# Two layers of cross-attention on one core: statistics between maxima and sums, a projection behind the first keys, and the last MLP two slots on

## The reference

```python
# layer 0
n = layernorm(x, ln1);  q, k, v = heads16(n @ wqkv)
r = x + merge(softmax(causal(q k^T / sqrt(128))) v) @ wproj + bproj
q2 = heads16(layernorm(r, ln2) @ ed_wq);  k2, v2 = heads16(layernorm(ctx, ln2) @ ed_wkv)
r = r + merge(softmax(q2 k2^T / sqrt(128)) v2) @ ed_wproj + ed_bproj
x = r + relu(layernorm(x, ln3) @ ff_w1 + ff_b1) @ ff_w2 + ff_b2
# layer 1: 16 heads of 64; keys are 16 memory tokens, 16 persistent ones and the 56 rows
x = x + attention(rope(q), rope(k), v) @ to_out_w
h = rmsnorm(x) @ ff_w1 + ff_b1;  a, g = split(h)
x = x + (silu(g) * a) @ ff_w2 + ff_b2
```

## Time and profile before

| | |
|---|---|
| median of 3 runs | 1267.42 us (1264.57 to 1268.15) |
| the profiled execution's own time | 1259.12 us |
| its span, first to last instruction | 1256.5 us |
| TensorE busy, mean granted clock | 1122.8 us (89%), 0.965 |
| VectorE, GpSimd, ScalarE busy | 910.4, 837.2, 752.5 us |

### The profile page before, as it was taken

How to read it: one execution, slowest core, us unless ns; L and a number is a source line. 1 busy time by engine, 2 the same in 40 slices (tenths; PEclk the granted TensorE clock), 3 DMA queues, 4 the chain that set the end, 5 groups by cost and what they waited for, 6 DMA issues and landing times. The chain is left out here.

```text
span 1256.5 us, 38139 instructions
## 1 busy us (share of the span) xinstructions
PE 1122.8 (89%) x15980; PEld 757.1 (60%) x15980; DVE 910.4 (72%) x1730; ACT 752.5 (60%) x1077; POOL 837.2 (67%) x1235
## 2 busy tenths in 40 slices
PE   2888878999999999999999999999657699898985
PEld 1555645666666666666666666666442457575663
DVE  6788757887787887778877788777356768686813
ACT  1333476777777777777777777777612336363641
POOL 2687467887888878878788787871009887767400
PEclk9999888999999999999999999999979899999987
DMA  7200043232222323223223232121000000000000
GB/s 172 85 2 1 17 127 109 72 108 87 94 96 83 107 77 105 98 70 118 79 95 109 66 113 89 64 76 39 2 17 1 2 2 2 8 2 1 9 9 8
DMA packets 70790, 75.99 MB, mean 60 GB/s; under 512 B 21596, under 2 KB 65372, under 8 KB 70492
## 3 DMA queue, kind: packets, MB, share of 16 engines
q1 hardware_dynamic: 70620, 73.57, 18.8%
HBM read 32.89 MB, written 0.92 MB: 27 GB/s over the span
## 5 line engine op out<-in xcount | busy, mean ns | idle before, releaser
L1129 DVE TENSOR_REDUCE tops_sb<-ps_b 112x2 f32<-112x1000 f32 x378 | 453.3, 1199 | 151.9 <-PE ps_b L899 149.5
L1054 ACT ACTIVATE probs_sb<-ps_a 128x896 f32<-128x896 f32 x352 | 322.6, 916 | 118.5 <-PE ps_a L851 118.5
L842 PE MATMUL ps_d<-probs_sb,values_sb 128*32 128x112 f32 x6144 | 228.2, 266 | 0.6 <-ACT probs_sb L1054 0.5
L899 PE MATMUL ps_b<-keys_sb,queries_sb 64*112 64x500 f16 x756 | 160.8, 416 | 14.4 <-DVE tops_sb L1129 9.4
L226 POOL TENSOR_SCALAR context_sb<-context_sb,ln_sb 125x128 f32<-125x128 f32 x384 | 168.4, 456 | 7.7 <-POOL ln_sb L244 7.6
L842 PEld LDWEIGHTS ps_d<-probs_sb,values_sb 128*32 128x32 f32 x6144 | 135.0, 109 | 40.2 <-issue 7.2
L851 PEld LDWEIGHTS ps_a<-queries_sb,keys_sb 64*128 64x128 f16 x3072 | 125.1, 102 | 49.9 <-ACT probs_sb L1054 8.7
L851 PE MATMUL ps_a<-queries_sb,keys_sb 64*128 64x112 f16 x3072 | 141.0, 210 | 5.8 <-ACT probs_sb L1054 5.5
L867 PE MATMUL ps_c<-xs_t_sb,w_kv_sb 128*128 128x200 f32 (+1 forms) x384 | 123.6, 419 | 0.9 <-ACT xs_t_sb L1079 0.9
L938 PE MATMUL ps_c<-w_kv_sb,xs_t_sb 128*128 128x128 f32 x768 | 119.2, 292 | 1.1 <-ACT k_rows_sb L997 1.0
L761 POOL TENSOR_TENSOR k_split_sb<-k_rows_sb,k_split_sb 128x500 f16<-128x500 f32 x96 | 109.0, 1136 | 8.0
(11 more groups left out here) (267 smaller groups left out, 1902.6 us busy)
## 6 DMA issues: line engine op xcount, KB each, us to landing
keys_sb<-k_split_sb SPq DMA_DIRECT2D x288, 125.0 KB, 2.5
context_sb<-in_ctx SPq DMA_DIRECT2D x32, 750.0 KB
queries_sb<-q_split_sb SPq DMA_DIRECT2D x21, 112.0 KB, 5.8
keys_sb<-in_ones SPq DMA_DIRECT2D x3, 375.0 KB, 3.3
w_qk_sb<-in_w_qkv SPq DMA_DIRECT2D x1, 1024.0 KB, 11.5
queries_sb<-shift_sb SPq DMA_DIRECT2D x64, 1.8 KB
x_all_sb<-in_x SPq DMA_DIRECT2D x2, 448.0 KB
out<-y_sb SPq DMA_DIRECT2D x8, 112.0 KB
```

The costliest lines, as they stand in the source:

```text
L842: last = nc.tensor.matmul(o_bank[32 * (g % 4):32 * (g % 4) + 32, 112 * (g // 4):112 * (g // 4) + 112], values[r][:, k, g, :], probs[k % 2] ...
L899: last = nc.tensor.matmul(scan_of(b + d, n)[0:2 * T, 512 * e:512 * e + 500], queries_of(b + d, e, g), keys[(r + d) % 3][64 * e:64 * e + 64 ...
L1054: nc.scalar.activation(probs[s % 2][:].rearrange("p (e n) -> p e n", e=2), halves(ps_a[:, :]), ACT.Exp).then_inc(Q["probs_ready"], 1)
L1129: nc.vector.tensor_reduce(tops[(b + d) % 2][:, :, n // 3, n % 3], scan_of(b + d, n)[0:2 * T, :].rearrange("p (e n) -> p e n", e=2)[:, :, 0 ...
```

## The change

It does three things.

1. Stage 1: in each pass VectorE's statistics move from behind the normalised result to between the last row maximum and the first row sum.
2. Stage 2: in b = -2 `queries_made(0)` moves from ahead of slot 0 to slot 3 on TensorE, so behind the first three key products, and `queries_high(0)` moves on ScalarE from slot 2 to slot 5, behind all three `keys_out`. In b = -1 the scan of a slot now stands ahead of that slot's `rows_turn` or `queries_made`.
3. Stage 3: in the last round the MLP of round 2 runs two slots earlier (`EARLIER` = 2), on TensorE, ScalarE and VectorE.

```diff
@@ stage 1, VectorE, in the loop over passes
                                                         own_half.unsqueeze(1).unsqueeze(3).broadcast_to([128, 16 * U, 2, D0]),
                                                         ALU.mult).then_inc(S["v_ready"], 1)
+                        if i < 2:
+                            context_counted(i)
+                        else:
+                            rows_counted(2 * U * (i - 2), U * i)
+                        if i == NIT - 1:
+                            n = U * i
+                            rsqrt(ve, row_link, rstd[:, 0:n], meanvar[:, 0:n, 1], newton[:, 0:n], EPS0)
                         for u in range(U):
                             wait("e0_ready", u + 1)
                             ins = nc.vector.reduce_sum(s_sum[:, u, :], s0[u][:], AX.X)
...
-                        if i < 2:
-                            context_counted(i)
-                        else:
-                            rows_counted(2 * U * (i - 2), U * i)
-                        if i == NIT - 1:
-                            n = U * i
-                            rsqrt(ve, row_link, rstd[:, 0:n], meanvar[:, 0:n, 1], newton[:, 0:n], EPS0)
                         if i == NIT - 1:
                             rows_done(i)
@@ stage 2, TensorE
                         if b == -2:
                             rows_turn(0)
-                            queries_made(0)
                         for s in range(KT):
+                            if b == -2 and s == 3:
+                                queries_made(0)
+                            d = 2 if s in AHEAD else 1
+                            if has(d):
+                                scan(UNITS[s], d)
                             if b == -1 and s % 3 == 0 and s < 9:
                                 rows_turn(s // 3 + 1)
                             if b == -1 and s % 3 == 1 and s < 9:
                                 queries_made(s // 3 + 1)
-                            d = 2 if s in AHEAD else 1
-                            if has(d):
-                                scan(UNITS[s], d)
@@ stage 2, ScalarE
-                            if b == -2 and s == 2:
+                            if b == -2 and s == 5:
                                 queries_high(0)
-                            if b == -2 and s == 5:
                                 queries_low(0)
@@ stage 3
-            ROW_AT, Y_AT = 6, 15
+            ROW_AT, Y_AT, EARLIER = 6, 15, 2
@@ TensorE, and the same on ScalarE and (with mlp_normed) on VectorE
                             if i > 0:
-                                mlp(i - 1, n)
+                                mlp(i - 1, n + EARLIER * (i == NIT - 1))
```

More of the change, by code:

```diff
@@ L1749, in _ @@
                             if i > 0:
-                                mlp_normed(i - 1, n)
-                                mlp(i - 1, n)
+                                mlp_normed(i - 1, n + EARLIER * (i == NIT - 1))
+                                mlp(i - 1, n + EARLIER * (i == NIT - 1))
                     for n in range(16):
```

## The result

| | before | changed |
|---|---|---|
| median of 18 runs each, one chip | 1266.05 us | 1255.83 us |
| ratio, 95% interval | 1 | 0.9935 (0.9916 to 0.9954) |
| the changed kernel in a second comparison | 1 | 0.9913 (0.9881 to 0.9944) |
| profiled execution: its time, span, granted clock | 1259.12, 1256.5, 0.965 | 1257.92, 1256.0, 0.953 |

The two medians differ by 10.2 us; the ratio of 0.9935, which has the interval, makes 8.2. Weighted by their intervals the two comparisons make 0.9929 ± 0.0016, or 9.0 ± 2.1 us of 1266.

The account below looks back on a forecast made before the run. TensorE, busy 686 of 698 us, fills stage 2's full part, so time moves only in stage 1, the pipeline-filling calls and the end. 1.2 + 0.2 - 1.6 - 4.6 = -4.8 us, from 1267.42 to 1262.6; range 1258.5 to 1267.0.

Parts of the forecast that it names:

- The statistics, pass by pass: Stage 1: moving the statistics gains 1.3 us in passes 0 and 2 but costs in pass 1; sum +1.2 us.
- the keys of passes 1 and 3 released by ScalarE: Sign in stage 1: in the changed profile the widened keys there wait for ScalarE's copy.
- little idle time ahead of the sums: Sign in stage 1: VectorE idles no more than 0.7 us ahead of the fourth sum in passes 0 and 2.
- a wait of 6.98 us in pass 1: Sign in stage 1: VectorE idles some 6.9 us ahead of the twelve BN_STATS, released by GpSimd's last statistics instruction.
- Passes 0 and 2: Stage 1: keys start when they leave PSUM, statistics covered by idle time; -1.3 us each.
- The term for pass 1: Stage 1: VectorE's wait for GpSimd delays pass 2's scores; +2.5 us, between 1.5 and 4.0, pass 0's gain included.
- Queries and scans: Stage 2's filling calls: first queries +0.2 us, scans ahead of the rows in b = -1 -1.6 us.
- The last round: Stage 3: down projection starts 2.1 us earlier and runs 2.55 us faster at the full clock; -4.6 us.
- The slow down projection: Rival, last round: the down projection stays slow, giving 2.1 not 4.6; total -2.3 us, 1265.1; chance 0.21.
- the call b = -1: Rival, stage 2: the queries' own chain bounds this call, its 1.6 us falls away; total -3.2, 1264.2; chance 0.13.
- the long low clock in pass 2: Rival, stage 1: after pass 1's wait the low clock holds for all of pass 2; +4.7 us, 1272.1; chance 0.04.

Follow-up runs that it names:

- the kernel with ten products: Ten unread products put on TensorE into pass 1's wait for the normalised result, against the changed kernel; 0.9915 of before.
- the last round's kernel: Only the last round's MLP two slots earlier, against the kernel before; 0.9970 in the first run, 0.9940 in the second.
- balanced statistics: Changed kernel, statistics dealt out as first context, four rows, second context plus four rows; pass 3's behind the result: 0.9907 of before, 0.9891 with unread last-MLP products.
- the widening in turn: Kernel before with one wait more: GpSimd begins its share of the widened keys when VectorE has done its own; 1259.16 us, 0.9941.

## Why the prediction missed

**The statistics: the step that failed.** "The statistics, pass by pass" made +1.2 of them; alone they measure -2.8 ± 2.3, and between the down projections of pass 0 and pass 3 -2.64. The waits it named were right: the keys of passes 1 and 3 released by ScalarE, little idle time ahead of the sums (0.83 us in pass 0, just over the 0.7 named), a wait of 6.98 us in pass 1 (6.9 forecast). What was wrong is that it charged the low clock to the one wait that the change makes and put at nothing the low clock behind the waits that it shortens. Two gains were not in the sum.

- Passes 0 and 2 gain 1.94 us each (18.15 to 16.21), not 1.3. VectorE now comes to the widening just ahead of GpSimd, not in the midst of its row, and takes 2.14 instead of 2.82.
- The scores behind the waits. I had put the low stretch in pass 2's scores down and used it only for the price of the new wait; that the change would remove such stretches in the three passes stood nowhere. First scores to down projection fell from 11.68 to 10.63 on the mean, 3.2 us in three passes.

Together -1.94 - 1.94 - 3.2, and pass 1's 23.6 for a mean of 19.2, +4.4: -2.7, beside the -2.64 between the down projections.

The term for pass 1 came out by luck: the scores of pass 2 start 2.7 us later, for +2.5. The forecast let half of the chain behind the wait run low and gave 4.0 if all of it did. All of it did (0.50 from 88.00 to 94.60), but from the transposition to the scores that is 4.28 us and not the 5.4 that it had added up, since the rows overlap and the output projection takes 1.73, not 2.08; at the full clock, in the kernel with ten products, it is 2.36. And 0.65 of the 2.7 stands already at the down projection of pass 0 (44.31 for 43.66), ahead of the first widening that the change can bring forward. In the other three profiles of the new stage 1 the scores start 0.9 to 3.3 later than in before's.

**Queries and scans: right in kind, sized from a best case.** -1.4 forecast, -4.2 ± 2.1 measured in the time, -2.1 in the rows up to stage 3. In the profiles of before and after the two first scans lie 23.15 and 21.47 us apart, the forecast's 1.6. But the old order is dearer when the clock is low there, and the profile of before showed its best case. VectorE and then TensorE in the last round's kernel, second run, which has the old order here, and below them the granted clock of the stretch in that run and in the changed kernel:

```profile
184.85 1.20 DVE L1129 TENSOR_REDUCE tops_sb<-ps_b 112x2 f32<-112x1000 f32 x1 [1.48 <-PE ps_b L899]
188.78 1.20 DVE L1129 TENSOR_REDUCE tops_sb<-ps_a 112x2 f32<-112x1000 f32 x1 [2.73 <-PE ps_a L899]
```

```profile
183.13 1.09 PE L878 MATMUL ps_d<-const_sb,values_sb 128*128 128x128 f32 x4 [1.38 <-DVE values_sb L1098]
...
186.24 1.91 PE L884 MATMUL ps_d<-keys_sb,w_q_sb 128*128 128x512 f32 x2
```

```profile
172.00:199.00 27.00, 21.90 (x80) 10.97 (x81) 17.82 (x27) 16.27 (x33) 17.48 (x29) 0.68 0.30 96
```

```profile
170.60:192.20 21.60, 18.26 (x78) 9.46 (x78) 17.24 (x25) 15.59 (x31) 15.33 (x25) 0.78 0.38 119
```

Where a scan stands behind a transposition or a projection at 1.2 GHz (1.09 and 1.91 us, for 0.63 and 1.13 in the group after them), VectorE waits 1.48 and 2.73 us for it, for 0.78 and 1.13; the old order took 26.02 us at 0.68. The new one takes 21.47 at 0.78, below the 0.85 at which before's profile took 23.15. From the opening transposition to the first scan it is 15.54 in before's profile, but 17.3 to 18.1 in five of the eight with the old code; with the new one 15.0 to 15.8 in eight of ten, and 17.3 in the two with balanced statistics. Of all this 0.3 us is given back by the third element's first scan, and 2.2 at the end of stage 2.

**The last round: right.** 64.62 became 59.66 from the first values product to the end of the last output projection, -4.96 for -4.6: 2.1 from the slot, 2.55 from the down projection at full clock, 0.35 from the output projection, at full clock throughout (7.31 for 7.66). Behind it the last MLP ends another 0.65 us earlier (26.87 to 26.22), which I had called unchanged.

**The rivals.** The slow down projection did not come in any of the ten profiles with the new last round; the call b = -1 did what it is for up to the third element; the long low clock in pass 2 did not come: behind the 6.19 us wait it was over by the scores (1.09 us at 94.81). None of the rivals had more gain than the forecast. The sizes on that side came from one execution that stood 8.3 us below the median; I carried the difference over to the median and kept the sizes of a lucky run.

## What to carry to other kernels

In this kernel a wait on TensorE of 2.56 us or more cost its own length and, in 15 of 21 passes, another 1.6 us of scores at the low clock; when a change shortens a wait, count both, and count them in each place where it recurs. Measure a gain to the end of the stage behind it: a part of it can be lost where nothing was edited. Where a kernel's times scatter by more than the effect, one profile shows one draw: ask of each step how long it would take with the products in it at 1.2 GHz, and prefer the order in which the work that another engine waits for stands ahead of those products. Before adding work to an engine's idle time, look at what the other engines do at that moment: here one wait that keeps two engines apart was worth 7.5 us, the move of the statistics 2.8.

## What was unexpected of the hardware

VectorE and GpSimd hold each other up in the widening, and by how much depends on when VectorE arrives. The next rows give shortest, median and longest of two instructions of VectorE in ns: before in pass 1; the last round's kernel, first run, in pass 1; and with the widening in turn.

```profile
L596 DVE TENSOR_TENSOR k_wide_sb<-k_sb,const_sb x2: 1370/1448/1526, 89.1 to 90.4; 128x512 f32<-128x512 f32 x2
```

```profile
L596 DVE TENSOR_TENSOR k_wide_sb<-k_sb,const_sb x2: 679/3236/5792, 88.9 to 94.6; 128x512 f32<-128x512 f32 x2
```

```profile
L597 DVE TENSOR_TENSOR k_wide_sb<-k_sb,const_sb x2: 678/684/690, 85.3 to 85.9; 128x512 f32<-128x512 f32 x2
```

Alone the instruction takes 0.68 us. By the starts of both engines' instructions in all profiles, one that begins inside one of GpSimd's with 0.6 us or more left to GpSimd's next takes 1.2 to 1.5, and GpSimd's go from 1.04 to about 1.5 beside it; one with 0.16 to 0.20 left takes 5.75 to 6.79, to some 0.5 us past the end of GpSimd's whole row of six; one that begins 0.05 or less ahead of GpSimd's next takes 0.69 to 0.81. That goes with the 21.7 us instead of 18.15 behind the old code's pass 1 in all three profiles in which that pass's scores ran at the full clock: 1.6 us gained bring VectorE to the wrong moment, and the gain is lost twice over. The Trainium skill, "SBUF — State Buffer", section "Who interferes with whom", says that a VectorE instruction with two SBUF inputs contends with a GpSimd instruction that reads SBUF, and that the order of issue decides which of them blocks. The rows agree on the pair of instructions, and in the long holds VectorE's is the later one; but these last through a whole row of six of GpSimd's instructions, of which five or all six began after VectorE's. What decides that beyond the moment of arrival was not tried.
